# A decoder kernel on one core: ScalarE takes the fold copies of the cross attention, and the step lists are written anew

## What is computed

```python
def attention(x, w_q, w_k, w_v, w_o):              # 16 heads of 8, 4 K/V heads, causal
    q, k = rms(x @ w_q), rms(x @ w_k); v = x @ w_v # rms norm of each head
    q, k = rope(q), rope(k)
    s = tanh(q @ k.T / sqrt(8) / 50) * 50          # capped scores
    return softmax(where(causal, s, -inf)) @ v @ w_o

def cross(x, ctx, ...):                            # ctx: 4 x 32 x 96, 4 heads of 32
    s = (x @ Wq) @ (ctx @ Wk).T / sqrt(32), masked # top 32 of 32: a plain softmax
    c = mean_over_heads(softmax(s)) @ (ctx @ Wv) * text_mask
    h = layernorm(x) * (1 + gate * (c @ Wf_in)[:128] ...) + gate * shift_in
    y = causal_convolution(h, kernel(log_dt, A, C)) + h * D_skip      # S4D, by a DFT
    xt = x + (y * (1 + gate * scale_out) + gate * shift_out)
    return layernorm(xt + gelu(layernorm(xt) @ W1 + b1) @ W2 + b2)

def moe(x, ...):                                   # 2 shared experts and 8 routed, 2 of 8 a token
    shared = mean over 2 of gelu(x @ sW1 + sb1) @ sW2 + sb2
    gates = x @ rW + rb; the two best, softmax of the two
    return shared + sum over the chosen e of w_e * (gelu(x @ W1[e] + b1[e]) @ W2[e] + b2[e])

x = layernorm(x + attention(x)); x = layernorm(x + cross(x, ctx)); x = layernorm(x + moe(x))
```

## Time and profile before

| | |
|---|---|
| median of three runs | 554.73 us (553.6 to 555.08) |
| the profiled execution's own time, and its span | 553.21 us, 551.5 us |
| busy in the span: PE, DVE, ACT, POOL | 413.4, 373.3, 324.7, 258.1 us |
| mean granted clock of TensorE, of full speed | 0.889 |
| first tanh, last `oT` copy done | 50.07, 298.7 us |
| `place:3` done and the last scatter starts | 432.5 us |
| `by:45`, the last block's copy, done | 518.0 us |

### The profile page before, as it was taken

The page is one execution under the profiler, slowest core; times in us unless marked ns, Lnnn a source line. Parts: engine busy times, 40 slices in busy tenths (PEclk is TensorE's granted clock), DMA queues, the critical chain, the costliest instruction groups (busy, mean ns, idle before and its releaser), DMA issues.

```text
span 551.5 us, 9139 instructions
## 1 busy us (share of the span) xinstructions
PE 413.4 (75%) x2857; PEld 266.1 (48%) x2857; DVE 373.3 (68%) x1104; ACT 324.7 (59%) x561; POOL 258.1 (47%) x305
## 2 busy tenths in 40 slices
PE   3347356767468888799769995898989889788950
PEld 2124014335154333444235562467778778778830
DVE  1996789549996299947998897988645611652144
ACT  2018975998969789989883330723736444344410
POOL 2403786566853155814753465436172403720172
PEclk9987566888779889999798996999999989899995
DMA  3897000000018920000000000036957488899312
GB/s 100 175 370 311 1 2 1 6 6 1 5 22 187 168 72 1 1 2 2 1 0 1 26 15 0 10 108 212 287 169 222 160 287 245 279 283 311 93 49 57
DMA packets 45893, 58.56 MB, mean 106 GB/s; under 512 B 9627, under 2 KB 34966, under 8 KB 45846
## 3 DMA queue, kind: packets, MB, share of 16 engines
q1 hardware_dynamic: 37174, 50.78, 30.9%
q0 software_dynamic: 2048, 4.20, 2.7%
q10 hardware_dynamic: 6624, 3.02, 1.9%
HBM read 42.23 MB, written 20.46 MB: 114 GB/s over the span
## 4 chain that ended last, share of the span: by engine, by line
DVE 42%; PE 20%; issue 10%; POOL 8%; DMA 6%; ACT 6%; SPq 6%; DVEq 0%; POOLq 0%; ACTq 0%
POOL y_pair L1134 4%; SPq L477 3%; DMA x_blk<-expert_rows 3%; PE ring_g L781 3%; PE ring_s L854 2%; PE ring_g L862 2%; DVE stats L1383 2%; PE ring_g L753 2%; PE ring_g L786 2%; DMA y_pair<-expert_out,y_rows 2%; DVE hn L1394 2%; PE ring_g L583 2%; PE bank_o L703 2%; DVE g_raw L1544 2%; ACT probs L928 2%
## 5 line engine op out<-in xcount | busy, mean ns | idle before, releaser
L922 ACT ACTIVATE probs<-ring_s 128x512 f32<-128x512 f32 (+1 forms) x192 | 87.6, 540 | 15.4 <-PE ring_s L689 15.2
L971 ACT ACTIVATE g_ring<-ring_s,w_blk 128x128 f32<-128x128 f32 x184 | 52.1, 370 | 65.2 <-PE ring_s L854 44.6
L1080 POOL TENSOR_SCALAR_AFFINE_SELECT probs<-probs 128x256 f32<-128x256 f32 (+1 forms) x96 | 50.8, 559 | 58.5 <-ACT probs L928 58.5
L928 ACT ACTIVATE probs<-probs 128x2560 f32<-128x2560 f32 x32 | 75.1, 2346 | 0.8
L689 PE MATMUL ring_s<-qT,kT 64*128 64x512 bf16 (+3 forms) x256 | 52.2, 340 | 28.8 <-ACT probs L922 24.3
L1134 POOL DMA_INDIRECT y_pair<-expert_out,y_rows x32 | 30.9, 966 | 59.1 <-issue 38.5
L854 PE MATMUL ring_s<-xT_blk,w_blk 128*128 128x128 f32 x368 | 50.3, 283 | 3.3 <-DVE xT_blk L1691 3.2
L703 PE MATMUL bank_o<-probs,vv 128*32 128x128 f32 (+3 forms) x512 | 45.8, 506 | 8.0 <-POOL probs L1080 6.3
L1121 POOL DMA_INDIRECT expert_rows<-x,rows_i x32 | 31.3, 977 | 40.3 <-DVE rows_i L1670 31.8
L862 PE MATMUL ring_g<-w_blk,g_ring 128*128 128x128 f32 x368 | 48.6, 280 | 1.3 <-DVE xT_blk L1691 0.9
L854 PEld LDWEIGHTS ring_s<-xT_blk,w_blk 128*128 128x128 f32 x368 | 46.3, 198 | 6.6 <-issue 6.3
(11 more groups left out here) (339 smaller groups left out, 899.7 us busy)
## 6 DMA issues: line engine op xcount, KB each, us to landing
w_blk<-expert_pack SPq DMA_DIRECT2D x46, 578.0 KB, 4.6
expert_rows<-zero_rows SPq DMA_DIRECT2D x2, 4096.0 KB, 20.7
expert_pack<-in_L_ffn_W SPq DMA_DIRECT2D x16, 256.0 KB
x_blk<-expert_rows SPq DMA_DIRECT2D x46, 64.0 KB, 3.7
expert_out<-y_blk ACTq DMA_DIRECT2D x46, 64.0 KB, 4.2
x<-in_x SPq DMA_DIRECT2D x4, 256.0 KB, 3.6
...
```

The costliest lines, as they stand in the source:

```text
L922: f(probs[:, pair % NPROB, BASE[n]:BASE[n] + WIDTH[n]], s_bank("sc", b, p, n)[:, 0:WIDTH[n]], ACT.Tanh, scale=1.0 / (CAP * float(np.sqrt(n ...
L928: f(probs[:, pair % NPROB, :], probs[:, pair % NPROB, :], ACT.Exp, scale=CAP).then_inc(exp_done, 1)
L971: last = f(g_ring[:, u % RING, P * n:P * (n + 1)], s_bank("bu", k)[:, P * n:P * (n + 1)], ACT.Gelu, bias=w_blk[:, k % SLOTS, HID + n:HID + ...
L1080: last = g.affine_select(out=v, in_=v, compare_op=ALU.is_ge, fill=0.0, base=0, pattern=[[0, v.shape[1]], [1, P]], channel_multiplier=-1)
```

## The change

ScalarE gets five steps, `masks`, `fold1`, `fold2`, `fold3` and `fold4`, with the copies and scalings that VectorE made before; the conversion of the context mask goes to `bias`, the clearing of `kbd` to GpSimd's `begin`. `vectors` is left with two copies. Semaphores are added where a consumer now sits behind ScalarE (`rows_wide`, `ctx_spread`, `masks_ready`), and the first `scores` step waits for two of them. All four lists are new; no word of a product or of another step is added or dropped. Their beginnings:

```diff
 DVE_ORDER
-rms:0 vectors rroot:0 fold1 bias ctabs fold2 parts:0 fold3 steps copies:0 vv:0 fold4:0 fold4:1 states fold4:2 states2 ...
+rms:0 vectors rroot:0 bias steps vv:0 ctabs parts:0 states copies:0 states2 states3 pack rms:1 rroot:1 args:0.0 ...
 ACT_ORDER
-xT:0 qkv:0.0 qkv:0.1 xT:1 states qT:0.0 ...
+xT:0 qkv:0.0 qkv:0.1 masks fold1 xT:1 fold2 states fold3 fold4:0 fold4:1 fold4:2 fold4:3 qT:0.0 ...
```

And the code, cut to its core:

```diff
             def fold4(b):            # TensorE's
                 pe.wait_ge(*g_freed("fold2b"))
-                pe.wait_ge(pro_sb, 2)
+                pe.wait_ge(ctx_spread, 1)
...
+            def masks():
+                act.wait_ge(ld_cross, 16 * 11)
+                f(tm_rows[:, :], tm_rows8[:, :], ACT.Copy).then_inc(rows_wide, 1)
+                op(f(gate4[:, :], gate[:, :], ACT.Copy, scale=0.25))
+                for n in range(2):
+                    at = slice(2 * D * n, 2 * D * (n + 1))
+                    op(f(film_bias[:, at], film_bias[:, at], ACT.Copy, scale=gate[:, 0:1]))
+                then()
+                for n in range(2):
+                    at = slice(2 * D * n, 2 * D * n + D)
+                    last = f(film_bias[:, at], film_bias[:, at], ACT.Copy, bias=1.0)
+                last.then_inc(masks_ready, 1)
+            def fold1():
+                bank = g_bank("fold1")
+                act.wait_ge(g_full, g_done("fold1"))
+                f(wqT[:, :], bank[:, 0:P], ACT.Copy)
+                f(tmask[:, :], bank[:, 3 * P:3 * P + B * NT], ACT.Copy)
+                op(f(ctxT[:, :], bank[0:DV, P:2 * P], ACT.Copy))
+                f(wvT[:, :], bank[:, 2 * P:2 * P + DV], ACT.Copy).then_inc(g_freed("fold1")[0], 1)
+                then()
+                for h in range(XH):
+                    last = f(ctx_rep...[:, :, h, :], ctxT[:, :]..., ACT.Copy)
+                last.then_inc(ctx_spread, 1)
+            def fold2():
+                bank = g_bank("fold2a")
+                act.wait_ge(g_full, g_done("fold2a"))
+                act.wait_ge(blank_ready, 1)
+                for h in range(XH):
+                    last = f(kbd...[32 * h:32 * h + 32, :, h, :], bank[32 * h:32 * h + 32, 0:B * G]..., ACT.Copy)
+                last.then_inc(g_freed("fold2a")[0], 1)
+                act.wait_ge(g_full, g_done("fold2b"))
+                f(wvf[:, :], g_bank("fold2b")[0:DV, :], ACT.Copy).then_inc(g_freed("fold2b")[0], 1)
+            def fold3():
+                f(xq[:, :, :]..., g_bank("fold3")[:, :], ACT.Copy).then_inc(g_freed("fold3")[0], 1)
+            def fold4(b):
+                f(vf[:, b, :], g_bank("fold4", b)[:, :], ACT.Copy, scale=gate4[:, 0:1]).then_inc(...)
...
             def begin():             # GpSimd's
                 op(g.memset(zero_rows[:, :], 0.0))
+                g.memset(kbd[:, :], 0.0)
...
             def vectors():           # VectorE's
-                dve.wait_ge(ld_cross, 16 * 11)
-                v.tensor_copy(tm_rows[:, :], tm_rows8[:, :]).then_inc(pro_sb, 1)
-                one(v.memset(kbd[:, :], 0.0))
-                op(v.tensor_copy(cmask[:, :], cmask8[:, :]))
-                op(ts(gate4[:, :], gate[:, :], 0.25, None, ALU.mult))
-                one(ts(film_bias[:, :], film_bias[:, :], gate[:, 0:1], None, ALU.mult))
-                op(ts(cmask[:, :], cmask[:, :], 1.0, 3e38, ALU.subtract, ALU.mult))
-                for n in range(2):
-                    op(ts(film_bias[:, 2 * D * n:2 * D * n + D], ..., 1.0, None, ALU.add))
-                then()
...
             def bias():
-                then()
+                dve.wait_ge(ld_cross, 16 * 11)
+                one(v.tensor_copy(cmask[:, :], cmask8[:, :]))
+                one(ts(cmask[:, :], cmask[:, :], 1.0, 3e38, ALU.subtract, ALU.mult))
...
             def scores(b):
                 dve.wait_ge(g_full, g_done(f"xs:{b}", *([f"attnT:{b - 1}"] if b else [])))
+                if b == 0:
+                    dve.wait_ge(masks_ready, 1)
+                    dve.wait_ge(*g_freed("fold1"))
```

More of the change, by code:

```diff
@@ L149 @@
-store:39 bg:41 store:40 sg:3.0 store:41 bg:42 bg:43 bg:44 store:42 bg:45 store:43 store:44 store:45 sg:3.1 sg:3.2
-sg:3.3 sg:3.4 sg:3.5 sg:3.6 sg:3.7
+xT:0 qkv:0.0 qkv:0.1 masks fold1 xT:1 fold2 states fold3 fold4:0 fold4:1 fold4:2 fold4:3 qT:0.0 qT:0.1 qT:0.2 qT:0.3
+qT:0.4 qT:0.5 tanh:0.0.0 qkv:1.0 tanh:0.0.1 tanh:0.0.2 tanh:0.0.3 qkv:1.1 tanh:0.0.4 tanh:0.0.5 xT:2 exp:0 tanh:0.1.0
+tanh:0.1.1 tanh:0.1.2 decays:0 tanh:0.1.3 tanh:0.1.4 tanh:0.1.5 exp:1 tanh:0.2.0 tanh:0.2.1 tanh:0.2.2 tanh:0.2.3
@@ L151 @@
+sg:3.5 bg:41 bg:42 store:40 bg:43 store:41 bg:44 store:42 bg:45 store:43 store:44 store:45 sg:3.6 sg:3.7
 """
 DVE_ORDER = """
-rms:0 vectors rroot:0 fold1 bias ctabs fold2 parts:0 fold3 steps copies:0 vv:0 fold4:0 fold4:1 states fold4:2 states2
-states3 pack rms:1 fold4:3 rroot:1 args:0.0 args:0.1 args:0.2 parts:1 powers:0 args:1.0 copies:1 args:1.1 oT:0
-evac:0.0 args:1.2 y:0 evac:0.1 oT:1 args:2.0 powers:1 y:1 args:2.1 oT:2 evac:1.0 y:2 args:2.2 evac:1.1 args:3.0 vv:1
-powers:2 oT:3 args:3.1 y:3 rms:2 yT:0 rroot:2 args:3.2 proj:0 evac:2.0 evac:2.1 oT:4 powers:3 parts:2 x1:0 copies:2
@@ L172 @@
-fin:3.2 fin:3.3 fo:3
+rms:0 vectors rroot:0 bias steps vv:0 ctabs parts:0 states copies:0 states2 states3 pack rms:1 rroot:1 args:0.0
+args:0.1 args:0.2 parts:1 powers:0 args:1.0 oT:0 args:1.1 y:0 copies:1 evac:0.0 args:1.2 evac:0.1 oT:1 powers:1
+args:2.0 y:1 args:2.1 evac:1.0 oT:2 args:2.2 y:2 evac:1.1 powers:2 vv:1 args:3.0 oT:3 args:3.1 rms:2 y:3 rroot:2
+args:3.2 evac:2.0 evac:2.1 yT:0 proj:0 powers:3 x1:0 parts:2 oT:4 copies:2 evac:3.0 evac:3.1 scores:0 oT:5 xnorm:0 y:4
+y:5 tap xn:0 spectra soften:0 oT:6 y:6 film:0.0 film:0.1 film:0.2 film:0.3 mod:0 vv:2 oT:7 lags:0.0 lags:0.1 lags:0.2
@@ new lines @@
+y:7 shape:0 hnorm:0 yT:1 rms:3 h:0 rroot:3 proj:1 oT:8 hT:0 y:8 parts:3 x1:1 copies:3 xnorm:1 scores:1 oT:9 ffT:0
+soften:1 oT:10 ffn:0 y:9 xn:1 y:10 film:1.0 film:1.1 x2n:0 film:1.2 film:1.3 mod:1 x2:0 lags:1.0 oT:11 vv:3 lags:1.1
+y:11 lags:1.2 yT:2 shape:1 proj:2 hnorm:1 x1:2 oT:12 xnorm:2 h:1 y:12 gates:0 xn:2 route:0 oT:13 weights:0 scores:2
+hT:1 y:13 place:0 select:0 soften:2 oT:14 y:14 film:2.0 film:2.1 film:2.2 film:2.3 mod:2 lags:2.0 lags:2.1 lags:2.2
+oT:15 ffT:1 shape:2 y:15 ffn:1 yT:3 hnorm:2 proj:3 x2n:1 x1:3 x2:1 xnorm:3 h:2 settle:0 xn:3 scores:3 hT:2 gates:1
@@ L1726, in _ @@
             play(DVE_ORDER, {
[L1727 removed]
+                "vectors": vectors, "steps": step_sizes,
                 "states": states, "states2": states2, "states3": states3, "pack": pack, "args": args, "powers": powers, "evac": evacuate, "ctabs": conv_tables, "tap": first_tap,
```

235 lines of the change are left out of this document (104 added, 131 removed).

## The result

The changed kernel takes 548.91 us (median of four runs, 547.61 to 549.56) where the kernel before took 554.75 (553.60 to 555.08, four runs): a ratio of 0.990, 95% interval 0.9863 to 0.9937. It is faster by 5.8 us; forecast were 10.7, to 544.0, with a range of 534 to 556. The profiled execution took 549.56 us with a span of 547.7, so that the two profiles differ by 3.8 us of span, less than the medians.

A forecast was written before the change was run, and what follows sets the result against it. ScalarE was taken to hold the attention's pace, TensorE the stage to `place:3`, VectorE's chain the prologue. −7.0 + 6.8 − 15.0 + 4.5 = −10.7 us, from 554.7 to 544.0; range 534 to 556.

The forecast's parts named there:

- the blocks: Group 1's blocks after `place:3`: five more shared-expert units add 9 us, half into idle time, +4.5 us (bounds 0 to 9).
- the end: After the last block's copy: fetches decide it, products formerly behind the last block ran beside them; 33.5 us stay, 0 change.
- the attention: First tanh to last `oT`: added FFN and cross-attention work priced by ScalarE, +6.8 us (bounds 0 to 15.2).
- the prologue: Start to first tanh: VectorE work moved to ScalarE lets `qT` start earlier, −7.0 us (bounds 4.7 to 7.1 saved).
- the smaller gain: Rival: VectorE and GpSimd block each other over shared ports, 6.3 us more in three `lags`; −4.4 us, 550.3, chance 0.13.
- the test that I set for the sign: Last `oT` expected near 298.5; after 309.2 the kernel would be slower, past 310.9 measurably slower.
- From the last `oT` to `place:3`: Stage after attention: TensorE loses 15.1 us and VectorE 15.2 us of work, −15.0 us (bounds 13.4 to 17 saved).
- The slower case: Rival: VectorE's in-order queue in the attention's last third adds 15.2 us plus 6.3 for shared ports; +4.0, 558.7, chance 0.13.
- the two engines in each other's way: In the attention, VectorE and GpSimd lock shared SBUF ports: three `lags` take 5.2 us each, not 3.1, adding 6.3 us.

## Why the prediction was right, and where it wasn't

The sign held and the time, 548.9, lies in the range of 534 to 556. Of the five terms only the blocks and the end held; the other three were outside their bounds. The total is no further off because misses cancel: the attention cost 16.7 us more than forecast, and the stage behind it gave 8.1 more, the prologue 1.5 more. That is luck in part. The time is also just above the 539 to 548 that I gave one half, and nearer to the 550.3 of the smaller gain, though not by the mechanism named there. And the test that I set for the sign failed: the last `oT` ended at 313.7, past the 310.9 from which I called the kernel slower, and it is faster, since what the attention lost came back behind it. Point by point:

**The prologue**, −7.0, measured −8.5, beyond its bounds of 4.7 to 7.1. `rroot:0` starts at 13.3 (13.4 forecast), ScalarE's `states` at 24.3 (24.4 forecast), its folds are through at 29.6 (31), and neither `qT` waits for `vf`. `copies:0` ends at 33.5 instead of 34.7: `ctabs`, 2.9 us long before, took 1.6, and the four scalings of the context mask 1.4 instead of 3.0. The runs with the new prologue and the old lists show that nothing of this lead is lost in the attention (247.0, 248.9 and 249.2 us). On the slower chips this term is as good as the whole change. On the others that is shown only together with the units among the blocks.

**The attention**, +6.8, measured +23.5, outside the bounds of 0 to 15.2. This is the step that failed. I priced the added work by ScalarE, the fullest engine over the whole stretch, although it goes into the last third, where three engines were level. Even ScalarE's own price was low: its busy time rose by 9.9 us, not 6.8, since the three gelus of `su:0.0` to `su:0.2` and their change of table, 3.1 us, were not in my sum. In the last third the moved products stand on TensorE in order ahead of scores, and ScalarE's waits for scores rose from 15.4 to 34.7 us. TensorE's busy time up to the last `oT` rose by 21.1 us, more than the 15.1 that I moved: `su:0.3`, `ffT:1` and the three `conv:2` stand between `val:15` and the last `oT` too, because VectorE's queue has the `lags` of batch 2 ahead of it. `val:15` was done at 309.6, the copy started at 312.96; before the change these were 297.1 and 297.99. So by the end of `val:15` the stretch grew by 21.0 us and not 23.5; by the start of the last exp (288.4 and 302.8) it grew by 22.9.

**From the last `oT` to `place:3`**, −15.0, measured −23.1, outside 13.4 to 17. TensorE's work there fell by 19.0 us, by the same cut, and its idle time by 4.1. The two terms are one: together they were forecast −8.2 and measured +0.4. Here the work of TensorE that went from one stage to the one before was paid in full: its busy share was 88% in the last 72.7 us of the attention (63.9 busy), and 89% before in the stage that the work left. Over both stages TensorE's idle time fell by 1.9 us, and its work rose by 2.2 (302.8 to 305.0), which left the stretches behind (88.2 to 85.6).

**The blocks and the end**, +4.5 and 0, measured +4.5 and −0.2 in the result's profiles. The other chip of 554 us has profiles that agree with both (88.5 to 90.4 us with six units among the blocks, 83.2 with one; an end of 33.2 to 33.6). The 4.5 to the tenth is luck: five units were to bring 9 us of TensorE's work, half of it into idle time, and its work there rose by 6.3, its idle time fell by 1.8. On the two slower chips the premise that the units at the end run beside the fetches for nothing does not hold: there the end is 42.8 and 43.5 us with them in the changed kernel and 33.2 to 33.4 without, and the move gains.

**The rivals.** The slower case named VectorE's queue in the last third. It did what the text says of it in one place (`hT:1` behind `route:0`), but taking that away moved the attention's end by only 2.3 us and gained no time. By its own mark, a last `oT` past 310.9, it came true, and the time did not follow. Its other half, the two engines in each other's way, came true for other instructions than I said. The `lags` of batch 2 took 3.5, 3.1 and 3.1 us, not 5.2. `route:0` took 4.9 instead of 2.6: two of its products, and GpSimd's instructions beside them,

```profile
274.38 1.50 DVE L1612 TENSOR_TENSOR fb<-gates 128x256 f32<-128x256 f32 x1
275.92 1.38 DVE L1613 TENSOR_TENSOR fb<-fb,earlier 128x256 f32<-128x256 f32 x1
```

```profile
274.20 1.40 POOL L1143 TENSOR_TENSOR xn<-xn,norms 128x512 f32<-128x512 f32 x1 [0.41 <-DVE xn L1406]
275.68 1.34 POOL L1145 TENSOR_TENSOR xn<-xn,norms 128x512 f32<-128x512 f32 x1
```

and the same two in the run with `hT:1` earlier, where GpSimd is idle until 281.52, when its next instruction starts:

```profile
281.06 0.42 DVE L1612 TENSOR_TENSOR fb<-gates 128x256 f32<-128x256 f32 x1
281.51 0.43 DVE L1613 TENSOR_TENSOR fb<-fb,earlier 128x256 f32<-128x256 f32 x1
```

The table load's drain that the Trainium skill states ("ScalarE: Activation LUTs", What ACT_TABLE_LOAD costs) isn't there in the changed kernel either: the load at 288.58 takes 1.28 us and the gelu starts at 289.87.

What stays open: what the engines wait for while GpSimd issues its fetches on the slower chips (the fetches' own traffic, or their own instructions), and why these chips differ. That the fetches delay the blocks rests on one run, on a chip without such a stop; that they cause the stops rests on the times at which these end. Nor does a run say which of the moved steps make up the 23.5 us of the attention, beyond the 2.3.
